# Sparse expert stage of an attention and mixture-of-experts layer: a rolled loop over resident weights against written-out tiles with weights brought per tile

## The chip, the cores and the metric

One core of one Trainium2 chip runs the whole program in one launch. The metric is device time in microseconds (us), the median of three runs.

## The reference

Input x is 2 x 1024 tokens of 128 channels, float32. The first half of the layer is causal attention with 16 heads and a layer norm around it. The second half, where the change lies, sends each token to 2 of 7 experts and to one shared expert:

```python
x_flat = layernorm(x).reshape(-1, 128)                    # 2048 tokens
logits = x_flat @ router_w.T                              # 7 experts
top_vals, top_idx = top_k(logits, 2);  top_w = softmax(top_vals)
swiglu(x, wg, wu, wd) = (silu(x @ wg) * (x @ wu)) @ wd    # 128 -> 512 -> 128, per expert
mixed = sum over the token's 2 experts of top_w * swiglu(x, expert) + swiglu(x, shared)
x = x + layernorm(mixed)
```

## The kernel before

The first block (lines up to 835) does the attention, the layer norms and the first half of the routing; both kernels do it alike. It ends near 378 us in the profile. The second block holds the rest of the layer:

- **Shared expert and routing.** The shared expert runs over 4 chunks of 512 tokens (`shared_up`, `shared_take`, `shared_down`, `shared_result`). Beside it VectorE (DVE) ranks the 4096 (token, expert) pairs by expert and writes two tables: `source` (which token stands in row p of tile k) and `target` (where its result goes), each 128 x 38. There are 38 tiles of 128 rows, each wholly of one expert. Which expert a tile belongs to is packed in `words`, one number for six tiles, three bits each. `places_ready` says that the tables are there, `words_ready` that the words are.
- **Weights.** At the start of the block SyncE (SP) issues 24 DMAs of 256 KB: gate, up and down weights of the shared expert and of all seven others, into `w_g`, `w_u`, `w_d`, where they stay.
- **Expert tiles.** For tile k: GpSimd (POOL) gathers 128 token rows from `tokens` in HBM by an indirect DMA (`gather`). TensorE (PE) transposes them (`turn`, L1164), ScalarE (ACT) copies the result to `rows_t`. PE multiplies them by gate and up weights (`up`, L1182, L1185): `rows_t` stands in the array and 512 weight columns move, so `hidden` comes out with tokens on partitions. ACT takes the silu, DVE the product (`hidden`, L1537). PE transposes `hidden` in four pieces (`turn_hidden`, L1173), ACT copies it (L1300), and PE multiplies it by the down weights (`project`, L1195). DVE copies the 128 x 128 result (L1545), and POOL scatters it to `results` in HBM (`scatter`).
- **Loops.** Each engine has a rolled loop (`Fori`). PE turns through six tiles at a time, reads a word into a register and takes the weights at a register's offset. The order on PE for tile k is turn(k+2), turn_hidden(k), up(k+1), project(k). Rows, hidden and results have two buffers each.
- **POOL's loop.** An indirect DMA takes its 128 row numbers from a column of SBUF. Since the column's place depends on the loop, POOL first copies it to `source_now` or `target_now` (L1018, L1030), waits for its own copy on `copied`, and then issues the DMA (L1021, L1033). Its order is gather(k+4), scatter(k).
- **End.** When all results are stored, SP brings them back in eight DMAs, they are weighted and added, and the last layer norm and the residual follow.

Of the kernel before, what the change touches and what calls it, by code (L numbers as in the profile page):

```python
# [25 lines left out]
P = 128  # L26
# [25 lines left out]
TAIL = 2  # L52
assert (TILES - TAIL) % PACK == 0 and PACK % 2 == 0
# [65 lines left out]
def program(nc, x, wqkv, wq_t, dirs, scales, w_out, router_t, w_gate, w_up, w_down, out):  # L119
    ctx = ExitStack()  # L120
    with ctx:
# [715 lines left out]
        w_g = sb("w_g", [C, NE, HID])  # L837
        w_u = sb("w_u", [C, NE, HID])
        w_d = sb("w_d", [P, NE, HT, C])
# [45 lines left out]
        source_now = [sb(f"source_now{i}", [P, 1], U32) for i in range(2)]  # L885
        target_now = [sb(f"target_now{i}", [P, 1], U32) for i in range(2)]
        rows = [sb(f"rows{i}", [P, C]) for i in range(2)]
        rows_t = [sb(f"rows_t{i}", [C, P]) for i in range(2)]
        gate = [sb(f"gate{i}", [P, HID]) for i in range(2)]
        hidden = [sb(f"hidden{i}", [P, HID]) for i in range(2)]  # L890
        hidden_t = [sb(f"hidden_t{i}", [P, HT, P]) for i in range(2)]
        result = [sb(f"result{i}", [P, C]) for i in range(2)]
# [5 lines left out]
        experts_loaded = sem("experts_loaded")  # L898
# [23 lines left out]
        rows_loaded = [sem(f"rows_loaded{i}") for i in range(2)]  # L922
        copied = sem("copied")
        offsets_in_place = sem("offsets_in_place")
# [6 lines left out]
        hidden_turned = sem("hidden_turned")  # L931
        hidden_t_ready = sem("hidden_t_ready")
        down_done = sem("down_done")
        result_ready = sem("result_ready")
        result_stored = [sem(f"result_stored{i}") for i in range(2)]
# [11 lines left out]
        PAIRS = (TILES - TAIL) // 2  # L947
        LAST = TILES - TAIL

        with nc.Block() as block:  # L950
            at_bank, pr_bank = [bank(0), bank(1)], [bank(2), bank(3)]
            g_bank, u_bank = [bank(0), bank(1)], [bank(2), bank(3)]
            xt_bank = turn_bank = [bank(4), bank(5)]
            d_bank, t_bank = bank(6), bank(7)
            cut = NT * 8
# [3 lines left out]

            @block.sync  # L960
            def _(sp):

                for e in [E] + list(range(E)):
                    loaded = shared_loaded if e == E else experts_loaded
                    sp.dma_start(w_g[:, e, :], w_gate[e]).then_inc(loaded, 16)
                    sp.dma_start(w_u[:, e, :], w_up[e]).then_inc(loaded, 16)
                    sp.dma_start(w_d[:, e, :, :], w_down[e].rearrange("(t p) c -> p t c", p=P)
                                 ).then_inc(loaded, 16)
# [4 lines left out]
                for i in range(2):  # L973
                    sp.wait_ge(result_stored[i], 16 * (TILES // 2))
# [16 lines left out]
            def _(pool):  # L991
# [22 lines left out]
                def gather(pair, u, count):  # L1014

                    k, i = pair * 2 + u, u % 2
                    pool.wait_ge(rows_turned, k + 1)
                    nc.gpsimd.tensor_copy(source_now[i][:, :], source[:, bass.ds(k, 1)]).then_inc(copied, 1)  # L1018
                    pool.wait_ge(copied, count)
                    pool.sem_inc(offsets_in_place, 1)  # L1020
# [5 lines left out]
                def scatter(pair, u, count):  # L1026

                    k, i = pair * 2 + u, u % 2
                    pool.wait_ge(result_ready, k + 1 + 1)
                    nc.gpsimd.tensor_copy(target_now[i][:, :], target[:, bass.ds(k, 1)]).then_inc(copied, 1)  # L1030
                    pool.wait_ge(copied, count)
                    pool.sem_inc(offsets_in_place, 1)
                    nc.gpsimd.indirect_dma_start(  # L1033
                        results, bass.IndirectOffsetOnAxis(ap=target_now[i][:, 0:1], axis=0),
                        result[i][:, :], None).then_inc(result_stored[i], 16)
# [3 lines left out]
                AHEAD = 4  # L1039
                for u in range(AHEAD):  # L1040
                    gather(0, u, u + 1)
                with pool.Fori(0, PAIRS - 1) as pair:
                    for u in range(2):
                        gather(pair, u + AHEAD, pair * 4 + (AHEAD + 2 * u + 1))
                        scatter(pair, u, pair * 4 + (AHEAD + 2 * u + 2))
                for u in range(AHEAD):
                    scatter(PAIRS - 1, u, (PAIRS - 1) * 4 + AHEAD + u + 1)

# [13 lines left out]
            def _(pe):  # L1062
                pe.sem_inc(rows_turned, CREDIT)

# [29 lines left out]
                def shared_up(q, ts):  # L1094
                    x_at = x2_t[:, q * CH:(q + 1) * CH, :].rearrange("c t p -> c (t p)")
                    for t in ts:
                        if q == CHUNKS - 1 and t >= 2:
                            pe.wait_ge(s_last_ready, t - 1)
                        elif q * HT + t >= 2:
                            pe.wait_ge(s_up_ready, q * HT + t - 1)  # L1100
                        nc.tensor.matmul(g_bank[t % 2], w_g[:, E, t * P:(t + 1) * P], x_at,
                                         start=True, stop=True).then_inc(s_gate_done, 1)
                        nc.tensor.matmul(u_bank[t % 2], w_u[:, E, t * P:(t + 1) * P], x_at,
                                         start=True, stop=True).then_inc(s_up_done, 1)

                def shared_down(q):
# [6 lines left out]
                    for j in range(CH):  # L1113
                        for t in range(HT):
                            last = nc.tensor.matmul(  # L1115
                                d_bank[:, j * P:(j + 1) * P],
                                s_hidden[q % 2][:, t, j * P:(j + 1) * P], w_d[:, E, t, :],
# [35 lines left out]
                def word(turn):  # L1153
                    return pe.value_load(words[0:1, bass.ds(turn, 1)], min_val=0, max_val=8 ** (PACK + 1) - 1)

                def digit(w, u):
                    return (w >> (3 * u)) & 7

                def turn(k, u):

                    i = u % 2
                    pe.wait_ge(rows_loaded[i], k * 8 + (u // 2 + 1) * 16)
                    pe.wait_ge(rows_t_ready, k + (u + 1))
                    nc.tensor.transpose(t_bank[:, i * P:(i + 1) * P], rows[i][:, :], ident[:, :]  # L1164
                                        ).then_inc(rows_turned, 1)

                def turn_hidden(k, u):

                    i = u % 2
                    pe.wait_ge(hidden_ready, k + (u + 1 + CREDIT))  # L1170
                    pe.wait_ge(hidden_t_ready, k + (u + 1))
                    for t in range(HT):
                        last = nc.tensor.transpose(turn_bank[i][:, t * P:(t + 1) * P],  # L1173
                                                   hidden[i][:, t * P:(t + 1) * P], ident[:, :])
                    last.then_inc(hidden_turned, 1)

                def up(k, u, e):

                    i = u % 2
                    pe.wait_ge(rows_t_ready, k + (u + 1 + 1))  # L1180
                    pe.wait_ge(hidden_ready, k + (u + 1))
                    nc.tensor.matmul(g_bank[i], rows_t[i][:, :],  # L1182
                                     w_g[:, bass.ds(e, 1), :].rearrange("c e h -> c (e h)"),
                                     start=True, stop=True).then_inc(gate_done, 1)
                    nc.tensor.matmul(u_bank[i], rows_t[i][:, :],  # L1185
                                     w_u[:, bass.ds(e, 1), :].rearrange("c e h -> c (e h)"),
                                     start=True, stop=True).then_inc(up_done, 1)

                def project(k, u, e):

                    i = u % 2
                    pe.wait_ge(hidden_t_ready, k + (u + 1 + CREDIT))
                    pe.wait_ge(result_ready, k + (u + 1))
                    for t in range(HT):
                        last = nc.tensor.matmul(d_bank[:, 0:P], hidden_t[i][:, t, :],  # L1195
                                                w_d[:, bass.ds(e, 1), t, :].rearrange("p e c -> p (e c)"),
# [4 lines left out]
                turn(0, 0)  # L1201
                turn(0, 1)
                shared_down(CHUNKS - 1)
                pe.wait_ge(words_ready, 1)
                pe.wait_ge(experts_loaded, 16 * 3 * E)
                first_expert = digit(word(0), 0)
                up(0, 0, first_expert)
                pe.wait_ge(s_down_taken, CHUNKS)
                with pe.Fori(0, (TILES - TAIL) // PACK) as n:
                    w, k = word(n), n * PACK  # L1210
                    for u in range(PACK):
                        turn(k, u + 2)
                        turn_hidden(k, u)
                        up(k, u + 1, digit(w, u + 1))
                        project(k, u, digit(w, u))
                w = word(WORDS - 1)
                turn_hidden(LAST, 0)
                up(LAST, 1, digit(w, 1))
                project(LAST, 0, digit(w, 0))
                turn_hidden(LAST, 1)  # L1220
                project(LAST, 1, digit(w, 1))

# [390 lines left out]
```

## Time and profile before

| | |
|---|---|
| device time, median of 3 runs (lowest to highest) | 625.59 us (623.78 to 627.57) |
| profiled execution, first to last instruction | 621.6 us |
| mean granted TensorE clock, share of full speed | 0.950 |
| busy over the span: PE, DVE, ACT, POOL | 490.9, 356.5, 287.1, 141.3 us |
| DMA over the span | 27.38 MB, mean 44 GB/s |
| first gather issued; first matmul of tile 0 | 432.82 us; 441.40 us |
| last result of tile 37 copied; result DMAs read back from | 591.67 us; 595.34 us |

The times of the profile are from one profiled execution, in us from its first instruction. Its span is 4.0 us under the median of the runs, which also hold what lies around the first and last instruction. "PE" is TensorE's matmul track, "PEld" its weight loads. A float32 matmul shows as two PE instructions.

### The profile page before, as it was taken

To read this page: it belongs to the slowest core of one execution; us is meant where nothing else is said; L and a number is where in the kernel's file an instruction comes from. 1 tells how busy PE (TensorE), PEld (TensorE's weight loads), DVE (VectorE), ACT (ScalarE), POOL (GpSimd) and SP (SyncE) were. 2 spreads that over 40 slices of the span, in tenths; PEclk is the share of its full clock that TensorE was granted. 3 is DMA by queue.
4 is the path that set the end of the run, shared out by engine and by line. 5 is a ranking of instruction groups with operands and counts; after the bars stand their busy time and mean duration, and the time that the engine had idled before them with its cause. 6 is when DMAs were issued, how large, how long until landed. Compare 5 with 4: busy or idle time off the path is not lost. (4 is left out here: it accounts for less than half of the span.)

```text
span 621.6 us, 12143 instructions
## 1 busy us (share of the span) xinstructions
PE 490.9 (79%) x3660; PEld 261.3 (42%) x3661; DVE 356.5 (57%) x936; ACT 287.1 (46%) x639; POOL 141.3 (23%) x214
## 2 busy tenths in 40 slices
PE   1636789898994999989898987888888889888800
PEld 0421234443442434444443445555555556555500
DVE  4966988686873767868673662688222212222247
ACT  0330045665753657565575765752333333333321
POOL 9310000000000000000000001424365556655424
PEclk9987889999998999999999997999999999999965
DMA  3066030210303003030000005900011111111152
GB/s 89 4 152 152 1 55 3 39 18 7 50 4 57 2 3 55 3 53 4 3 1 3 2 1 181 294 1 4 21 33 34 34 33 30 34 34 34 25 143 67
DMA packets 31930, 27.38 MB, mean 44 GB/s; under 512 B 7723, under 2 KB 25516, under 8 KB 31852
## 3 DMA queue, kind: packets, MB, share of 16 engines
q1 hardware_dynamic: 29444, 21.71, 15.2%
q0 software_dynamic: 2432, 4.99, 3.0%
q8 instruction: 29, 0.48, 0.3%
q14 instruction: 25, 0.20, 0.1%
HBM read 18.55 MB, written 7.73 MB: 42 GB/s over the span
## 5 line engine op out<-in xcount | busy, mean ns | idle before, releaser
L703 DVE TENSOR_REDUCE mx_part<-banks 128x1 f32<-128x512 f32 (+3 forms) x384 | 194.9, 552 | 79.0 <-PE banks L426 38.9
L608 ACT ACTIVATE probs<-banks 128x512 f32<-128x512 f32 (+3 forms) x384 | 164.6, 496 | 134.9 <-PE banks L445 134.2
L426 PE MATMUL banks<-k_st,q_st 128*128 128x512 bf16 (+3 forms) x384 | 126.8, 341 | 24.7 <-DMA k_st<-k_parts 13.7
L441 PE MATMUL banks<-q_st,k_st 128*128 128x512 bf16 (+3 forms) x384 | 117.2, 332 | 9.4 <-ACT probs L608 4.5
L463 PE MATMUL banks<-probs,v_pad 128*32 128x256 f32 (+1 forms) x1280 | 95.4, 370 | 13.0 <-ACT probs L608 13.0
L1537 DVE TENSOR_TENSOR hidden<-banks,gate 128x512 f32<-128x512 f32 x38 | 26.3, 691 | 108.9 <-PE banks L1185 108.9
L426 PEld LDWEIGHTS banks<-k_st,q_st 128*128 128x128 bf16 x384 | 37.4, 98 | 82.8 <-DVE mx_part L703 43.7
L441 PEld LDWEIGHTS banks<-q_st,k_st 128*128 128x128 bf16 x384 | 36.9, 97 | 68.5 <-ACT probs L608 46.3
L359 POOL COPY v_pad<-v_all 128x256 f32 (+1 forms) x8 | 3.7, 479 | 246.4 <-PE banks L463 229.7
L429 PE MATMUL banks<-mask_qk,ident_b 128*128 128x128 bf16 x256 | 56.2, 224 | 0.0
L445 PE MATMUL banks<-mask_kq,ident_b 128*128 128x128 bf16 x256 | 52.8, 220 | 0.0
L1195 PEld LDWEIGHTS banks<-w_d,hidden_t 128*128 128x128 f32 x304 | 39.8, 191 | 18.7 <-issue 18.7
L463 PEld LDWEIGHTS banks<-probs,v_pad 128*32 128x32 f32 x1280 | 25.3, 107 | 49.3 <-ACT probs L608 24.4
L1033 POOL DMA_INDIRECT results<-result,target_now x38 | 37.7, 993 | 31.0 <-POOL target_now L1030 31.0
L1021 POOL DMA_INDIRECT rows<-tokens,source_now x38 | 38.0, 999 | 30.0 <-POOL source_now L1018 26.0
L1288 ACT ACTIVATE rows_t<-banks 128x128 f32<-128x128 f32 x38 | 10.5, 278 | 72.2 <-PE banks L1164 72.2
L1195 PE MATMUL banks<-w_d,hidden_t 128*128 x304 | 40.1, 275 | 0.8 <-ACT hidden_t L1300 0.8
L1182 PE MATMUL banks<-w_g,rows_t 128*128 x76 | 40.6, 616 | 0.0
L1185 PE MATMUL banks<-w_u,rows_t 128*128 x76 | 38.8, 592 | 0.0
L1164 PE MATMUL banks<-ident,rows 128*128 128x128 f32 x38 | 12.0, 315 | 21.4 <-DMA rows<-tokens,source_now 21.3
L1295 ACT ACTIVATE gate<-banks 128x512 f32<-128x512 f32 x38 | 22.7, 597 | 11.7 <-PE banks L1182 11.7
L1300 ACT ACTIVATE hidden_t<-banks 128x512 f32<-128x512 f32 x38 | 22.7, 597 | 10.7 <-PE banks L1173 10.7
(202 smaller groups left out, 550.3 us busy)
## 6 DMA issues: line engine op xcount, KB each, us to landing
q_st<-q_parts SPq DMA_DIRECT2D x48, 64.0 KB
w_g<-in_w_gate SPq DMA_DIRECT2D x8, 256.0 KB, 5.4
w_u<-in_w_up SPq DMA_DIRECT2D x8, 256.0 KB, 5.6
w_d<-in_w_down SPq DMA_DIRECT2D x8, 256.0 KB, 5.9
back<-results SPq DMA_DIRECT2D x8, 256.0 KB, 5.0
q_parts<-probs SPq DMA_DIRECT2D x12, 128.0 KB, 3.3
k_parts<-probs SPq DMA_DIRECT2D x12, 128.0 KB, 3.3
k_st<-k_parts SPq DMA_DIRECT2D x8, 192.0 KB
```

What stands on the lines that cost most here:

```text
L426: last = nc.tensor.matmul(dst[:, 0:z - a], q_st[r][:, h, i * P:(i + 1) * P], k_st[r][:, h, a:z], start=True, stop=(z < width))
L429: last = nc.tensor.matmul(dst[:, z - a - P:z - a], ident_b[:, :], mask_qk[:, :], start=False, stop=True)
L441: last = nc.tensor.matmul(dst[:, 0:z - a], k_st[r][:, h, j * P:(j + 1) * P], q_st[r][:, h, j * P + a:j * P + z], start=True, stop=(a > 0))
L445: last = nc.tensor.matmul(dst[:, 0:P], ident_b[:, :], mask_kq[:, :], start=False, stop=True)
L463: last = nc.tensor.matmul(o_bank[c][h * HQ:(h + 1) * HQ, a - c * BANK:z - c * BANK], v_pad[r][:, j, h, :], probs[j % 2][:, h, a - j * P:z ...
L608: nc.scalar.activation(probs[j % 2][:, h, a:z], score_bank[k % RING][:, 0:z - a], ACT.Exp).then_inc(slot_taken, 1)
L703: nc.vector.tensor_reduce(mx_part[r][:, h * KT + i, s:s + 1], max_bank[k % RING][:, 0:z - a], AX.X, ALU.max).then_inc(max_taken, 1)
L1021: nc.gpsimd.indirect_dma_start(rows[i][:, :], None, tokens, bass.IndirectOffsetOnAxis(ap=source_now[i][:, 0:1], axis=0)).then_inc(rows_loa ...
L1033: nc.gpsimd.indirect_dma_start(results, bass.IndirectOffsetOnAxis(ap=target_now[i][:, 0:1], axis=0), result[i][:, :], None).then_inc(resul ...
L1182: nc.tensor.matmul(g_bank[i], rows_t[i][:, :], w_g[:, bass.ds(e, 1), :].rearrange("c e h -> c (e h)"), start=True, stop=True).then_inc(gat ...
L1185: nc.tensor.matmul(u_bank[i], rows_t[i][:, :], w_u[:, bass.ds(e, 1), :].rearrange("c e h -> c (e h)"), start=True, stop=True).then_inc(up_ ...
L1195: last = nc.tensor.matmul(d_bank[:, 0:P], hidden_t[i][:, t, :], w_d[:, bass.ds(e, 1), t, :].rearrange("p e c -> p (e c)"), start=(t == 0), ...
```

## The change

The 38 tiles are written out on every engine instead of looped. What each part does:

- SP loads only the shared expert's weights at the start of the block (`s_w_g`, `s_w_u`, `s_w_d`). After `words_ready` it reads each tile's expert number into a register and issues three DMAs of 256 KB per tile into one of three sets of fixed buffers. The set of tile k is written again once project(k-3) is done (`down_done`). Before up(k), PE waits for all three of the tile.
- The offsets of gathers and scatters are read in place from `source` and `target`; the copies and their waits are gone. Rows and results have four buffers. POOL's order is gather(k+3), scatter(k), after the first four gathers.
- In `up` the weights stand and the rows move: four 128 x 128 matmuls for gate, four for up. `hidden` comes out with hidden units on partitions, so `turn_hidden` and ACT's copy are gone.
- The order on PE for tile k is turn(k+2), up(k+1), project(k). The turned rows and the results have two banks each.

```diff
+        w_d = [sb(f"w_d{i}", [P, HT, C]) for i in range(WEIGHTS)]      # WEIGHTS = 3, ROWS = 4
...
             def _(sp):
-                for e in [E] + list(range(E)):
-                    loaded = shared_loaded if e == E else experts_loaded
-                    sp.dma_start(w_g[:, e, :], w_gate[e]).then_inc(loaded, 16)
...
+                sp.wait_ge(words_ready, 1)
+                for k, e in enumerate(digits(sp)):
+                    i = k % WEIGHTS
+                    if k >= WEIGHTS:
+                        sp.wait_ge(down_done, k - WEIGHTS + 1)
+                    sp.dma_start(w_g[i][:, :], w_gate[bass.ds(e, 1), :, :].rearrange("e c h -> c (e h)")
+                                 ).then_inc(weights_in[i], 16)
+                    sp.dma_start(w_u[i][:, :], w_up[bass.ds(e, 1), :, :].rearrange("e c h -> c (e h)")
+                                 ).then_inc(weights_in[i], 16)
+                    sp.dma_start(w_d[i][:, :, :], w_down[bass.ds(e, 1), :, :].rearrange(
+                        "e (t p) c -> p (e t) c", p=P)).then_inc(weights_in[i], 16)
...
-                def gather(pair, u, count):
-                    k, i = pair * 2 + u, u % 2
-                    pool.wait_ge(rows_turned, k + 1)
-                    nc.gpsimd.tensor_copy(source_now[i][:, :], source[:, bass.ds(k, 1)]).then_inc(copied, 1)
-                    pool.wait_ge(copied, count)
+                def gather(k):
+                    i = k % ROWS
+                    if k >= ROWS:
+                        pool.wait_ge(rows_turned, k - ROWS + 1)
                     nc.gpsimd.indirect_dma_start(
                         rows[i][:, :], None, tokens,
-                        bass.IndirectOffsetOnAxis(ap=source_now[i][:, 0:1], axis=0)
+                        bass.IndirectOffsetOnAxis(ap=source[:, k:k + 1], axis=0)
                     ).then_inc(rows_loaded[i], 16)
+                def scatter(k):
+                    i = k % ROWS
+                    pool.wait_ge(result_ready, k + 1)
                     nc.gpsimd.indirect_dma_start(
+                        results, bass.IndirectOffsetOnAxis(ap=target[:, k:k + 1], axis=0),
                         result[i][:, :], None).then_inc(result_stored[i], 16)
...
+                for k in range(ROWS):
+                    gather(k)
+                for k in range(TILES):
+                    if ROWS <= k + ROWS - 1 < TILES and k > 0:
+                        gather(k + ROWS - 1)
+                    scatter(k)
...
+                def up(k):
+                    i = k % WEIGHTS
+                    pe.wait_ge(weights_in[i], 48 * (k // WEIGHTS + 1))
+                    pe.wait_ge(rows_t_ready, k + 1)
+                    if k >= 2:
+                        pe.wait_ge(hidden_ready, k - 1)
+                    for w, dst, sem_done in ((w_g, g_bank, gate_done), (w_u, u_bank, up_done)):
+                        for t in range(HT):
+                            last = nc.tensor.matmul(dst[k % 2][:, t * P:(t + 1) * P], w[i][:, t * P:(t + 1) * P],
+                                                    rows_t[k % 2][:, :], start=True, stop=True)
+                        last.then_inc(sem_done, 1)
...
+                turn(0)
                 shared_down(CHUNKS - 1)
+                turn(1)
                 pe.wait_ge(words_ready, 1)
+                up(0)
                 pe.wait_ge(s_down_taken, CHUNKS)
+                for k in range(TILES):
+                    if k + 2 < TILES:
+                        turn(k + 2)
+                    if k + 1 < TILES:
+                        up(k + 1)
+                    project(k)
```

## Rows read from the trace of the kernel before

**Rows 1.** Windows: PE, PEld, DVE, ACT, POOL busy us (instructions), clock, DMA share, GB/s.
```profile
459.00:579.00 120.00, 102.75 (x515) 68.20 (x515) 29.50 (x60) 44.33 (x91) 71.96 (x121) 1.00 0.12 33
```

**Rows 2.** Chain that ended last, around 514 us: start, duration, what.
```profile
513.94 0.21 POOL source_now L1018
...
514.19 0.52 issue
...
514.93 2.52 DMA rows<-tokens,source_now
...
517.57 0.34 PE banks L1164
```

**Rows 3.** Timeline from 447 us, one tile on PE: start, duration, idle before.
```profile
447.33 0.27 PE L1164 MATMUL banks<-ident,rows 128*128 128x128 f32 x1
...
447.45 0.66 PE L1173 MATMUL banks<-ident,hidden 128*128 128x128 f32 x4
...
447.95 1.04 PE L1182 MATMUL banks<-w_g,rows_t 128*128 x2
...
449.68 1.05 PE L1195 MATMUL banks<-w_d,hidden_t 128*128 x8
...
450.57 0.27 PE L1164 MATMUL banks<-ident,rows 128*128 128x128 f32 x1
...
450.77 0.29 DVE L1545 COPY result<-banks 128x128 f32<-128x128 f32 x1
```

**Rows 4.** SP's own issues in time: weights at 378 us, register-addressed attention loads, results back.
```profile
378.44 0.37 SPq L965 DMA_DIRECT2D w_g<-in_w_gate  x1
...
379.33 0.43 SPq L967 DMA_DIRECT2D w_d<-in_w_down  x1
...
117.96 2.37 SPq L278 DMA_DIRECT2D q_st<-q_parts  x6
...
595.34 0.36 SPq L978 DMA_DIRECT2D back<-results  x1
...
596.29 0.51 SPq L978 DMA_DIRECT2D back<-results  x1
```

**Rows 5.** DMA view, single issues: the first w_g, the first w_d, the third back.
```profile
w_g<-in_w_gate SPq DMA_DIRECT2D x1, 256.0 KB, 2.9
...
w_d<-in_w_down SPq DMA_DIRECT2D x1, 256.0 KB, 5.0
...
back<-results SPq DMA_DIRECT2D x1, 256.0 KB, 4.2
```

**Rows 6.** DMA view, 378 to 386 us (instruction queue) and 380 to 402 us.
```profile
q8 instruction: 1, 0.02, 0.7%
...
DMA packets 8550, 7.30 MB, mean 332 GB/s; under 512 B 413, under 2 KB 6530, under 8 KB 8546
```

**Rows 7.** Tile view of rows: issue of a gather to its landing.
```profile
DMA to landing us min/median/max: 2.5/2.6/3.5
```

**Rows 8.** Timeline, 431 to 438 us: tables ready, first copy, words, last shared chunk.
```profile
431.72 0.19 POOL L1018 COPY source_now<-source 128x1 uint32<-128x1 uint32 x1 [6.97 <-issue]
...
432.85 0.17 DVE L1521 CAST words<-words_f 1x7 uint32<-1x7 f32 x1
...
435.91 0.69 DVE L1476 TENSOR_TENSOR s_hidden<-banks,s_gate 128x512 f32<-128x512 f32 x1 [1.38 <-ACT s_gate L1253]
...
437.81 3.75 PE L1115 MATMUL banks<-w_d,s_hidden 128*128 128x128 f32 x32
```

**Rows 9.** Timeline, end of the tiles: the last result, and POOL behind it.
```profile
591.67 0.29 DVE L1545 COPY result<-banks 128x128 f32<-128x128 f32 x1 [2.23 <-PE banks L1195]
592.03 0.18 POOL L1030 COPY target_now<-target 128x1 uint32<-128x1 uint32 x1 [0.56 <-DVE result L1545]
```

**Rows 10.** Windows of 4 us: where the granted clock fell, and a stalled tile.
```profile
374.00:378.00 4.00, 1.79 (x8) 1.39 (x8) 0.62 (x2) 1.84 (x5) 0.00 (x0) 0.68 0.00 0
...
458.00:462.00 4.00, 2.98 (x15) 2.00 (x16) 0.34 (x1) 1.47 (x3) 2.40 (x5) 1.00 0.12 33
```

More of the change, by code:

```diff
@@ L51 @@
 PADDED = (WORDS + 1) * PACK
-TAIL = 2
-assert (TILES - TAIL) % PACK == 0 and PACK % 2 == 0
+WEIGHTS = 3
+ROWS = 4
 CH = BANK // P
@@ L832, in program @@
         front.close()
-        w_g = sb("w_g", [C, NE, HID])
-        w_u = sb("w_u", [C, NE, HID])
-        w_d = sb("w_d", [P, NE, HT, C])
+        s_w_g = sb("s_w_g", [C, HID])
+        s_w_u = sb("s_w_u", [C, HID])
+        s_w_d = sb("s_w_d", [P, HT, C])
+        w_d = [sb(f"w_d{i}", [P, HT, C]) for i in range(WEIGHTS)]
+        w_g = [sb(f"w_g{i}", [C, HID]) for i in range(WEIGHTS)]
+        w_u = [sb(f"w_u{i}", [C, HID]) for i in range(WEIGHTS)]
         proj = sb("proj", [P, KT, C])
@@ L884, in program @@
         s_hidden = [sb(f"s_hidden{i}", [P, HT, BANK]) for i in range(2)]
-        source_now = [sb(f"source_now{i}", [P, 1], U32) for i in range(2)]
-        target_now = [sb(f"target_now{i}", [P, 1], U32) for i in range(2)]
-        rows = [sb(f"rows{i}", [P, C]) for i in range(2)]
+        rows = [sb(f"rows{i}", [P, C]) for i in range(ROWS)]
         rows_t = [sb(f"rows_t{i}", [C, P]) for i in range(2)]
         gate = [sb(f"gate{i}", [P, HID]) for i in range(2)]
-        hidden = [sb(f"hidden{i}", [P, HID]) for i in range(2)]
-        hidden_t = [sb(f"hidden_t{i}", [P, HT, P]) for i in range(2)]
-        result = [sb(f"result{i}", [P, C]) for i in range(2)]
+        hidden = [sb(f"hidden{i}", [P, HT, P]) for i in range(2)]
+        result = [sb(f"result{i}", [P, C]) for i in range(ROWS)]
         root_table = sb("root_table", [P, 1])
@@ L921, in program @@
         s_down_taken = sem("s_down_taken")
-        rows_loaded = [sem(f"rows_loaded{i}") for i in range(2)]
-        copied = sem("copied")
-        offsets_in_place = sem("offsets_in_place")
+        weights_in = [sem(f"weights_in{i}") for i in range(WEIGHTS)]
+        rows_loaded = [sem(f"rows_loaded{i}") for i in range(ROWS)]
         rows_turned = sem("rows_turned")
@@ L958, in program, with digits @@
             rank_bank = t_bank[:, 2 * P + 3 * TILES:2 * P + 3 * TILES + E * NT]
+            def digits(engine):
+                for n in range(WORDS):
+                    word = engine.value_load(words[0:1, n:n + 1], min_val=0, max_val=8 ** (PACK + 1) - 1)
+                    for u in range(min(PACK, TILES - n * PACK)):
+                        yield (word >> (3 * u)) & 7
             @block.sync
             def _(sp):
-                for e in [E] + list(range(E)):
-                    loaded = shared_loaded if e == E else experts_loaded
-                    sp.dma_start(w_g[:, e, :], w_gate[e]).then_inc(loaded, 16)
-                    sp.dma_start(w_u[:, e, :], w_up[e]).then_inc(loaded, 16)
-                    sp.dma_start(w_d[:, e, :, :], w_down[e].rearrange("(t p) c -> p t c", p=P)
-                                 ).then_inc(loaded, 16)
+                sp.dma_start(s_w_g[:, :], w_gate[E]).then_inc(shared_loaded, 16)
+                sp.dma_start(s_w_u[:, :], w_up[E]).then_inc(shared_loaded, 16)
+                sp.dma_start(s_w_d[:, :, :], w_down[E].rearrange("(t p) c -> p t c", p=P)
+                             ).then_inc(shared_loaded, 16)
                 for b in range(B):
@@ L1038, in _ @@
                 pool.wait_ge(places_ready, 2)
[L1039 to L1047, printed above, removed]
+                for k in range(ROWS):
[4 more added lines that the diff above has]
+                    scatter(k)
                 for q in range(QC, CHUNKS):
@@ L1116, in shared_down @@
                                 d_bank[:, j * P:(j + 1) * P],
[L1117 removed]
+                                s_hidden[q % 2][:, t, j * P:(j + 1) * P], s_w_d[:, t, :],
                                 start=(t == 0), stop=(t == HT - 1))
@@ L1151, in _ @@
                 shared_up(3, [1, 2, 3])
[L1153 to L1164, printed above, removed]
-                                        ).then_inc(rows_turned, 1)
@@ L1167, in turn_hidden @@
[L1167 to L1171, printed above, removed]
-                    for t in range(HT):
[L1173 to L1196, printed above, removed]
+                def turn(k):
+                    i = k % ROWS
+                    pe.wait_ge(rows_loaded[i], 16 * (k // ROWS + 1))
+                    if k >= 2:
+                        pe.wait_ge(rows_t_ready, k - 1)
+                    nc.tensor.transpose(turn_bank[k % 2][:, 0:P], rows[i][:, :], ident[:, :]
+                                        ).then_inc(rows_turned, 1)
@@ L1197, in project @@
+                def project(k):
+                    pe.wait_ge(hidden_ready, k + 1)
+                    if k >= 2:
+                        pe.wait_ge(result_ready, k - 1)
+                    for t in range(HT):
+                        last = nc.tensor.matmul(down_bank[k % 2][:, 0:P], hidden[k % 2][:, t, :],
+                                                w_d[k % WEIGHTS][:, t, :],
                                                 start=(t == 0), stop=(t == HT - 1))
@@ L1200, in _ @@
                 pe.wait_ge(places_ready, 2)
-                turn(0, 0)
-                turn(0, 1)
+                pe.wait_ge(x2_t_ready, CHUNKS)
+                turn(0)
                 shared_down(CHUNKS - 1)
+                turn(1)
                 pe.wait_ge(words_ready, 1)
-                pe.wait_ge(experts_loaded, 16 * 3 * E)
-                first_expert = digit(word(0), 0)
-                up(0, 0, first_expert)
+                up(0)
                 pe.wait_ge(s_down_taken, CHUNKS)
[L1209 to L1221, printed above, removed]
+                for k in range(TILES):
[4 more added lines that the diff above has]
+                    project(k)
             @block.scalar
             def _(act):
-                act.sem_inc(rows_t_ready, 1)
-                act.sem_inc(hidden_t_ready, CREDIT)
                 for half in range(2):
@@ L1531, in _, with multiply, take_result @@
                                         ).then_inc(weight_ready, 1)
-                def multiply(pair, u):
-                    k, i = pair * 2 + u, u % 2
+                def multiply(k):
                     dve.wait_ge(gate_ready, k + 1)
                     dve.wait_ge(up_done, k + 1)
-                    nc.vector.tensor_tensor(hidden[i][:, :], u_bank[i], gate[i][:, :], ALU.mult
-                                            ).then_inc(hidden_ready, 1)
-                def take_result(pair, u, first=False):
-                    k, i = pair * 2 + u, u % 2
-                    dve.wait_ge(down_done, k + 1)
-                    if not first:
-                        dve.wait_ge(result_stored[i], pair * 16)
-                    nc.vector.tensor_copy(result[i][:, :], d_bank[:, 0:P]).then_inc(result_ready, 1)
-                multiply(0, 0)
-                for u in range(2):
-                    multiply(0, u + 1)
-                    take_result(0, u, first=True)
-                with dve.Fori(1, PAIRS) as pair:
-                    for u in range(2):
-                        multiply(pair, u + 1)
-                        take_result(pair, u)
-                multiply(PAIRS, 1)
-                for u in range(2):
-                    take_result(PAIRS, u)
+                    if k >= 2:
+                        dve.wait_ge(down_done, k - 1)
+                    nc.vector.tensor_tensor(hidden[k % 2][:, :, :].rearrange("p t n -> p (t n)"), u_bank[k % 2],
+                                            gate[k % 2][:, :], ALU.mult).then_inc(hidden_ready, 1)
+                def take_result(k):
+                    i = k % ROWS
+                    dve.wait_ge(down_done, k + 1)
+                    if k >= ROWS:
+                        dve.wait_ge(result_stored[i], 16 * (k // ROWS))
+                    nc.vector.tensor_copy(result[i][:, :], down_bank[k % 2][:, 0:P]).then_inc(result_ready, 1)
+                multiply(0)
+                for k in range(TILES):
+                    if k + 1 < TILES:
+                        multiply(k + 1)
+                    take_result(k)
                 dve.wait_ge(s_down_taken, CHUNKS)
```

71 lines of the change are left out of this document (25 added, 46 removed).

## The prediction

> **What bounds the kernel now.** I read the windows first. In the steady part of the tiles no engine looks full: PE is busy 103 of 120 us, POOL 72, DMA 12% [rows 1]. Busy share alone would name PE. The chain that ended last says otherwise: it runs through POOL's copy, an "issue" stretch and the indirect DMA, over and over, and PE appears only for a transpose released by a landed gather [rows 2]. The reader should see a latency loop inside POOL: copy starts 513.94, indirect DMA starts 514.93, so 0.99 us pass before the DMA's own 1.00 us. Two such per tile (gather, scatter) make 3.98 us, and 120 us / 3.98 is 30 tiles, the count of POOL's 121 instructions over four. The stretch of 0.52 us is POOL's sequencer preparing the indirect DMA. It cannot run ahead now, because it waits for the copy.
>
> PE alone needs less. Where gathers were ahead, a tile took it 450.57 - 447.33 = 3.24 us [rows 3]: transpose of rows 0.12, of hidden 0.50, gate and up 1.73, down 0.89. So POOL costs 0.75 us a tile over PE, and that is all that freeing POOL alone could give: 28 us over 38 tiles.
>
> **The change, part by part.**
>
> POOL. Without copies the sequencer can prepare one indirect DMA while the other executes, so POOL's own floor is two executions, 2.0 us a tile. Preparation still counts where POOL was waiting: from the end of the copy to the start of the DMA, 514.93 - (513.94 + 0.21) = 0.78 us [rows 2].
>
> PE. `turn_hidden` goes: -0.50. `up` becomes 8 float32 matmuls of 128 columns. Such a matmul costs 0.89 / 4 = 0.22 us in `project` (449.68 to 450.57) [rows 3], so 8 cost 1.78 against 1.73. Per tile 0.12 + 1.78 + 0.89 = 2.79 us. ACT loses a copy off the path. Nothing moves to DVE.
>
> The gather's round trip. gather(k+4) is issued behind scatter(k), and turn(k+4) is PE's next instruction after project(k+1). Call P(k) the end of project(k). DVE starts its copy 1.09 us after project's start, so P + 0.20, and takes 0.29 [rows 3]. Then 592.03 - 591.96 = 0.07 for the semaphore [rows 9], 0.78 preparation, 1.00 for the scatter, then gather to the transpose 517.57 - 514.93 = 2.64 [rows 2]. Together 0.20 + 0.29 + 0.07 + 0.78 + 1.00 + 2.64 = 4.98. Then turn, up and project, 2.79. So P(k+2) is at least P(k) + 7.77: two tiles per round trip.
>
> The weights' round trip. This is new, and SP, which issued nothing here, now issues 114 DMAs. The three of tile k+3 start when P(k) is seen, and up(k+3) comes after P(k+1) and the turn. Behind that waiting PE instruction stand project(k+2), and behind it DVE's copy and POOL's scatter. The loop is 0.20 + 0.07, then L, the time from the first issue to the third landing, 0.13 to wake PE, up and project 2.67: 3.07 + L per two tiles. L is the disputed number. From the first weights: first issued 378.44 [rows 4], third issued 379.33 and landed 5.0 later [rows 5], L = 5.9. In that time a block of instructions passed through one of the 16 DMA engines and held it 0.7% x 16 x 8 us = 0.9 us [rows 6], so undisturbed it would have been about 5.0. From the results read back at the end: third issued 596.29, landed 4.2 later, from 595.34: L = 5.15 [rows 4, 5], in smaller pieces. From below: the first DMA lands 2.9 after issue [rows 5], and 256 KB at the sustained 332 GB/s is 0.79 us [rows 6], so 2.9 + 2 x 0.79 = 4.5. I take 4.9, nearest to the undisturbed load, and 0.1 for the scatter that shares the engines: 3.07 + 5.0 = 8.07, say 8.05 per two tiles, 4.03 a tile. Register-addressed issue adds nothing visible: six such took 2.37 us, 0.39 each, no more than the static ones [rows 4]. Bandwidth is no bound: 3 x 0.79 = 2.4 us of 4 and the row traffic at 12% of 4 us, 0.5.
>
> On L the Trainium skill speaks for the change. Its page "DMA: Bandwidth & Descriptors", section "Anatomy of one DMA", fits a DMA from GpSimd as about 2.0 us plus bytes at 436 GB/s. By it the three, issued within 0.9 us, would be down after some 3.8 us, and the weights would never set the pace. The first w_g took 2.9 where the rule gives 2.6; the third disagrees more.
>
> Start. words is ready at 433.02 [rows 8]; 9 DMAs go out, and the first set lands by about 433.1 + 4.9 = 438, hidden behind the last shared chunk. The first gather starts about 0.4 us sooner (no copy), and `shared_down` no longer waits for the second gather: it starts when DVE's last product is there, 435.91 + 0.69 = 436.6 instead of 437.81 [rows 8]. 32 instructions at 0.11 end at 440.2; then turn(1) and up(0) to 442.1; turn(2), up(1), project(0): P(0) = 442.1 + 2.79 = 444.95. P(1) is 2.8 later.
>
> Middle. P(36) = 444.95 + 18 x 8.05 = 589.85; the last project follows directly, 0.95 later: P(37) = 590.8. Before, DVE's last copy started at 591.67 [rows 9], so P(37) was 591.47: -0.7.
>
> End. One copy and its wait less before the last scatter, -0.2.
>
> Instruction blocks. Written-out code is fetched once through the same DMA engines. A block held one engine 0.9 us [rows 6]. I estimate up to 15 blocks; each can delay one set of weights, on one of two interleaved chains (odd and even tiles), and only if it falls in the 2.4 of 4 us when they move: between 0 and 7 us, I take +1.5.
>
> Everything else in the block is unchanged. The 21 resident loads that go from 380 to 402 us stood beside a chain on DVE that did not wait for them: 0.
>
> Sum: -0.7 - 0.2 + 1.5 = +0.6 on 621.6, 622.2; with the 4.0 us by which the median of the runs stands above the profiled span, 626.2. I say 626.5.
>
> **The rivals.**
>
> Faster: the loads come down in under 4.6 us, and the gathers' round trip of 7.77 paces the stage. P(37) = 444.95 + 18 x 7.77 + 0.95 = 585.8, so -5.7 - 0.2 on the median: 619.7. For it: the lower bound of 4.5, and bursts that no longer queue behind 20 others. Against it: both observed L are above 5. A leaner preparation of the indirect DMA (0.5 instead of 0.78) would give 5 us more.
>
> Slower, one mechanism: the three loads take 5.9 us as observed, because gathers, scatters and instruction blocks share their engines each time. 3.07 + 5.9 = 8.97; P(37) = 445.9 + 161.5 = 607.4, +15.9 - 0.2: 641.3. It decides from L = 5.2 (8.27 and the 1.5 give more than 3.1 us). Gathers have landed as late as 3.5 us against a median of 2.6 [rows 7], so single DMAs do vary by 1 us.
>
> Clock: PE would be busy 5.6 of 8 us, 70%, with gaps of over 2 us. The granted clock fell where PE was busy 1.79 of 4 us, and not where it was busy 2.98 of 4 around a 2 us gap [rows 10]. At half clock a tile costs PE 5.6 us, 36 x 5.6 = 201: some 57 us more, 684. Unlikely.
>
> PE-bound: both round trips hidden, 2.79 a tile: 36 x 2.79 = 100 instead of 145, 580. The gather rows exclude it nearly.
>
> Loops: the skill's page "Runtime: NRT & Kernel Launch", section "Instruction fetch mechanics", says that a taken branch can force a fetch and that writing out avoids it. Here the loops' turns cost nothing on the path, as POOL held its 3.98 us throughout.
>
> **How the numbers follow.** A difference of 0.5%, 3.1 us, is about what a measurement can tell from no change. My case (weights' round trip, 7.9 to 8.3 us per two tiles; 622 to 631 us) 0.47, of it 0.05 faster, 0.32 same, 0.10 slower. Gather-paced 0.22, slow loads 0.27, clock 0.03, PE-bound 0.01. Faster 0.28, same 0.32, slower 0.40. The range 617.5 to 641 takes in the leaner gather partly and L up to 5.9; the likeliest case alone is 622 to 631.
>
> **What would show it.** After: no L1018 or L1030 copies, indirect DMAs of one tile back to back on POOL, POOL busy near half; PE waits before the first `up` matmul released by a w_d landing, every second tile (waits before the transpose by rows would mean the gathers pace); windows in which DMA is 65 to 75% busy at about 225 GB/s; first to third landing 4.9 to 5.1; 8.05 us per two tiles. The prediction is wrong if the third load lands outside 4.6 to 5.2 us, if the two weight DMAs of neighbouring tiles queue on each other, or if the clock drops.

## The result and the profile after

The changed kernel takes 659.59 us (median of 4 runs, 659.41 to 665.79) against 625.06 of before, measured beside it: ratio 1.0571, 95% interval 1.0523 to 1.062. It is 5.7% slower, outside the stated range of 617.5 to 641. The profiled execution spans 657.6 us, 36.0 more than before and 35.4 more than the 622.2 of the prediction's sum.

Windows of 20 us of the changed kernel, columns as in [rows 1]:

```profile
480.00:500.00 20.00, 14.87 (x100) 14.49 (x100) 3.68 (x9) 3.50 (x8) 7.78 (x8) 0.83 0.59 178
500.00:520.00 20.00, 14.68 (x100) 14.49 (x100) 3.84 (x8) 3.50 (x8) 7.59 (x9) 0.83 0.58 177
```

A tile has 25 PE instructions (1 + 16 + 8), so 100 in 20 us are four tiles: 5.0 us a tile, against POOL's 3.98 of before. The granted clock is 0.83, where it was 1.00 [rows 1]. Neither PE, nor POOL, nor DMA (0.59) is full.

The chain that ended last, one turn of it:

```profile
487.12 0.30 DVE result L1509
487.42 0.27 issue
487.69 0.99 POOL results L1037
488.67 0.30 issue
488.98 3.50 DMA rows<-tokens,source
492.48 0.04 issue
492.52 0.33 PE banks L1157
492.85 3.19 PE banks L1169 x16
496.05 1.14 PE banks L1178 x8
497.18 0.02 issue
497.21 0.30 DVE result L1509
```

This is the gathers' round trip, link by link: result copied, scatter, gather, landing, turn, `up`, `project`. It takes 497.21 - 487.12 = 10.09 us and moves two tiles. The weights do not appear in it. The timeline of the same stretch:

```profile
486.92 0.27 PE L1157 MATMUL banks<-ident,rows 128*128 128x128 f32 x1
487.02 1.06 PE L1169 MATMUL banks<-rows_t,w_g 128*128 128x128 f32 x8
...
492.52 0.33 PE L1157 MATMUL banks<-ident,rows 128*128 128x128 f32 x1 [2.66 <-DMA rows<-tokens,source]
...
492.69 1.65 PE L1169 MATMUL banks<-rows_t,w_g 128*128 128x128 f32 x8
...
494.13 1.91 PE L1169 MATMUL banks<-rows_t,w_u 128*128 128x128 f32 x8
```

The reader should see two things. PE idles 2.66 us in front of every second transpose, released by landed rows. And the eight instructions that took 1.06 us in the first tile take 1.65 to 1.91 in the tile after the gap. Windows of a few us show why:

```profile
489.00:492.50 3.50, 0.87 (x8) 0.68 (x7) 0.98 (x2) 0.00 (x0) 2.66 (x3) 1.00 1.02 325
492.50:496.00 3.50, 3.48 (x18) 3.48 (x19) 0.00 (x0) 0.88 (x2) 0.24 (x1) 0.57 0.55 174
496.00:499.00 3.00, 3.00 (x27) 3.00 (x26) 0.98 (x2) 0.87 (x2) 0.99 (x1) 0.93 0.09 16
```

In the first, PE is idle and the DMA engines are completely busy (1.02): the weights of a tile are moving while the rows wait for their turn. In the second, PE works at a granted clock of 0.57, that is, mostly at 1.2 GHz. In the third it is back near 2.4 GHz and the DMA engines are nearly idle (0.09). So the mean DMA share of 0.59 hides bursts at 100%, and the gather is issued into the burst.

The landing times, from the tile views of rows, w_g and w_d (issue to landing; [rows 5, 7] for before):

```profile
DMA to landing us min/median/max: 2.7/3.6/5.7
...
DMA to landing us min/median/max: 2.5/2.9/4.0
...
DMA to landing us min/median/max: 3.4/3.9/5.8
```

Rows land 1.0 us later than before (2.6). The third weight DMA is issued 0.9 us behind the first (490.11 and 491.01 in the timeline), so first issue to third landing is 4.8 us.

### The profile page after: what moved, and what is told of

Same layout as the page of the kernel before. It is cut to its first block and busy times, and to the rows that moved or that the text cites. A ratio compares the mean times of both kernels' runs of the same rounds, so it can differ in the third digit from the quotient of the medians.

```text
span 657.6 us, 12058 instructions
## 1 busy us (share of the span) xinstructions
PE 500.3 (76%) x3964; PEld 310.3 (47%) x3964; DVE 354.8 (54%) x936; ACT 264.3 (40%) x601; POOL 125.1 (19%) x138
## 5 line engine op out<-in xcount | busy, mean ns | idle before, releaser
L1037 POOL DMA_INDIRECT results<-result,target x38 | 37.5, 986 | 111.6 <-DVE result L1509 111.3
L1262 ACT ACTIVATE rows_t<-banks 128x128 f32<-128x128 f32 x38 | 10.5, 278 | 117.4 <-PE banks L1157 117.4
L1169 PE MATMUL banks<-rows_t,w_u 128*128 128x128 f32 x304 | 52.0, 329 | 0.0
L1169 PE MATMUL banks<-rows_t,w_g 128*128 128x128 f32 x304 | 47.9, 309 | 2.3 <-DMA w_d<-in_w_down 2.3
L1157 PE MATMUL banks<-ident,rows 128*128 128x128 f32 x38 | 12.5, 328 | 48.3 <-DMA rows<-tokens,source 48.3
L1169 PEld LDWEIGHTS banks<-rows_t,w_u 128*128 128x128 f32 x304 | 48.5, 243 | 0.0
L1178 PE MATMUL banks<-w_d,hidden 128*128 128x128 f32 x304 | 47.2, 307 | 0.0
L1169 PEld LDWEIGHTS banks<-rows_t,w_g 128*128 128x128 f32 x304 | 43.9, 222 | 2.9 <-DMA w_d<-in_w_down 2.7
L1178 PEld LDWEIGHTS banks<-w_d,hidden 128*128 128x128 f32 x304 | 44.7, 226 | 0.1
L1029 POOL DMA_INDIRECT rows<-tokens,source x38 | 36.9, 972 | 20.6 <-issue 11.3
```

What stands on the lines that cost most here:

```text
L1029: nc.gpsimd.indirect_dma_start(rows[i][:, :], None, tokens, bass.IndirectOffsetOnAxis(ap=source[:, k:k + 1], axis=0)).then_inc(rows_loaded ...
L1037: nc.gpsimd.indirect_dma_start(results, bass.IndirectOffsetOnAxis(ap=target[:, k:k + 1], axis=0), result[i][:, :], None).then_inc(result_s ...
L1169: last = nc.tensor.matmul(dst[k % 2][:, t * P:(t + 1) * P], w[i][:, t * P:(t + 1) * P], rows_t[k % 2][:, :], start=True, stop=True)
L1178: last = nc.tensor.matmul(down_bank[k % 2][:, 0:P], hidden[k % 2][:, t, :], w_d[k % WEIGHTS][:, t, :], start=(t == 0), stop=(t == HT - 1))
```

## The experiments

A is the theory that the weight traffic delays the gathers, B that the granted clock makes up the loss, C that the weights' round trip paces. E1 to E4 ran on one chip, E5, E6, E9 and E10 on one, E11 and E12 on one. E1, E2, E3, E5, E6 and E12 have one time each; their spans are compared with the 657.6 of the changed kernel. How far single runs scatter is seen from the kernel before, whose 21 runs beside the experiments took 619.96 to 629.16 us, with medians of 623.66, 624.78 and 624.42 on the three chips; a few us of one run are no finding by themselves. The time of the tiles alone, at the end of this section, scatters less.

**E1: no weight DMAs after tile 2.**

```diff
                     if k >= WEIGHTS:
-                        sp.wait_ge(down_done, k - WEIGHTS + 1)
+                        break
...
-                    pe.wait_ge(weights_in[i], 48 * (k // WEIGHTS + 1))
+                    pe.wait_ge(weights_in[i], 48)
```

> Left out: the weight DMAs of tiles 3 to 37 (the buffers keep the weights of tiles 0 to 2, so the results are of the wrong expert). Two tiles now take 10.1 us, 5.65 from the end of a project to the transpose of the rows four tiles on, and 4.45 for transpose, up and project. Theory A (the gathers share the DMA engines with the weights): landing falls from 3.6 to 2.6 us, the wait to 4.65; two tiles take 9.1 if the clock still falls each time, 7.5 if it no longer does: 640 or 611 us of span. Theory B (only the clock): landing stays 3.6, no gain unless the clock stays up. Theory C (the weights' own round trip paces): the wait on the weights goes, about the same gain as A, but the landing of the rows stays 3.6.

Measured: 627.61 us, span 625.6, 32.0 less. The rows' median landing is 2.7 us. Its chain:

```profile
503.44 0.30 DVE result L1509
503.75 0.27 issue
504.01 0.98 POOL results L1037
505.00 0.30 issue
505.30 2.53 DMA rows<-tokens,source
507.84 0.04 issue
507.88 0.33 PE banks L1157
508.21 1.79 PE banks L1169 x16
510.00 0.91 PE banks L1178 x8
510.91 0.02 issue
510.93 0.30 DVE result L1509
```

The same links take 510.93 - 503.44 = 7.49 us. Landing fell from 3.50 to 2.53, and `up` from 3.19 to 1.79: with the shorter gaps the clock mostly stays up (0.96 from 470 to 590 us). A holds and C falls, for the path still runs through the rows. The gain lies between the two cases that A gave, as some turns still lose the clock: behind its four gaps of 2.01 to 2.37 us the next tile took PE 4.23 to 4.48 us, behind those of up to 1.77 us about 3.0.

**E2: filler matmuls in PE's gap.**

```diff
                 for k in range(TILES):
+                    if 0 < k < TILES - 2:
+                        for _ in range(5):
+                            nc.tensor.matmul(turn_bank[k % 2][:, 2 * P:3 * P], ident[:, :], x2_t[:, 0, :],
+                                             start=True, stop=True)
                     if k + 2 < TILES:
                         turn(k + 2)
```

> Added: five float32 matmuls of 128 columns (1.1 us at full clock) in front of each rows transpose, into an unused part of a bank. They fit in the gap of 2.7 us that PE has in every second tile, and add nothing to what the path needs: 2 x (2.79 + 1.1) = 7.8 is under the present 10.1. Theory B (the granted clock halves because PE stands idle, and that costs 1.7 us per two tiles): clock 1.00 through the stage, two tiles take 5.65 + 2.79 = 8.45, span 657.6 - 18 x 1.65 = 628. Theory A alone (the clock does not matter): no gain, or 1.1 us lost per tile where PE was not waiting.

Measured: 638.87 us, span 637.1, 20.5 less with more work. The window from 470 to 590 us:

```profile
470.00:590.00 120.00, 108.54 (x939) 105.44 (x939) 26.55 (x54) 23.63 (x54) 51.50 (x53) 1.00 0.66 205
```

The clock is 1.00. B holds in kind, but the gain is 1.1 us per two tiles and not 1.65: the rows' landings in its chain from 490 to 515 us are 3.24, 4.67, 3.40 and 4.60 us (mean 4.0), against 3.62, 4.57, 3.17, 3.58, 3.50 and 3.93 (mean 3.7) in the changed kernel's chain from 447 to 500 us. More is moved in the same time (205 GB/s against 181 in the same window of the changed kernel); that this is what lengthens the landings is argued, no run shows it alone.

**E5: both.** No weight DMAs after tile 2, and the filler.

> Left out: the weight DMAs of tiles 3 to 37 (results of the wrong expert); added: the filler matmuls. Both costs named by A and B are then gone: rows land in 2.6 us and the clock is full. The gathers' round trip is 0.2 + 0.3 + 0.27 + 1.0 + 0.3 + 2.6 + 2.8 = 7.5 us per two tiles, PE with filler 7.8: span 616 to 620. If a third cost is at work, it stays at 625 or more.

Measured: 618.75 us, span 617.0, as expected. PE with its filler now sets the pace: from one transpose of rows to the next are 3.91 us in most turns, and PE waits for rows only five times. So the two costs together are worth at least 657.6 - 617.0 = 40.6 us. They are not additive (32.0 + 20.5 = 52.5), because the clock falls on account of the gap that the late rows make. No third cost is needed to explain this time; one hidden under PE's 3.91 us would not show.

**E3: eight row and result buffers.**

```diff
-ROWS = 4
+ROWS = 8
```

> Eight row and result buffers in place of four, so a gather is issued seven tiles ahead. Theory A+B (the round trip scatter to gather to transpose paces): PE no longer waits for rows; what is left is the weights' round trip, 3.07 + 4.8 = 7.9 us per two tiles at full clock, 9.5 with the clock falling: 618 to 646. Theory C (weights pace now): no change, 658.

Measured: 646.38 us, span 643.6, 14.0 less. The waits from 460 to 540 us (who waits <- for whom: us in all, times, the longest in us):

```profile
PE banks L1169 <- DMA w_d<-in_w_down: 20.7, 10, 3.3
```

PE no longer waits for rows; it waits for the third weight DMA. The path that I had forecast is real, but lies just behind the one that paced. The chain also holds one piece of 7.72 us from 436.26 for which no releaser is named, in front of the first `up`; E4 has more of that kind.

**E6: the gather in front of the scatter.** Four buffers as in the changed kernel.

```diff
-                    if ROWS <= k + ROWS - 1 < TILES and k > 0:
-                        gather(k + ROWS - 1)
+                    if k + ROWS < TILES:
+                        gather(k + ROWS)
                     scatter(k)
```

> One line of POOL's order changed: the gather of tile k+4 is issued before the scatter of tile k, not behind it. Buffers stay four and three. If the gather is late only because it stands behind a scatter that waits for the result, PE no longer waits for rows and the kernel falls to the pace of the weights' round trip, as with eight buffers: span 640 to 646. If four buffers are too few in themselves, it stays near 658.

Measured: 650.02 us, span 647.7, 9.9 less, near the expected 640 to 646 but not in it. From 490 to 530 us its chain holds landings of w_d and none of rows, and from 440 to 632 us PE waits 41.9 us for w_d and never for rows (48.3 us in the changed kernel). So the gathers came late for the scatter that they stood behind, which itself waited for a result.

**E12: eight buffers and the filler.**

> Eight row buffers and the filler matmuls: the gathers are off the path and the clock is held, so the weights' round trip of the prediction stands alone. By it, 3.07 us plus the first-to-third landing (4.8 in the changed kernel, 5.2 with eight buffers): 7.9 to 8.3 us per two tiles, span 622 to 629. If the round trip is longer than its parts, or PE waits elsewhere, it stays near 643.

Measured: 636.46 us, span 634.7, missed by 6 us. The clock is 1.00, and PE waits only for w_d, now as the chain shows:

```profile
482.69 0.02 issue
...
483.90 4.78 DMA w_d<-in_w_down
488.68 0.04 issue
488.72 2.05 PE banks L1169 x16
490.77 0.91 PE banks L1178 x8
```

This turn is 491.68 - 482.69 = 8.99 us: 483.00 to 488.68 for the three DMAs (5.7 where the medians give 5.0), and 2.05 + 0.91 for PE after a wait where I had 1.78 + 0.89. In the mean a turn takes 8.7 us (17 turns in 148.16 us). The weights' round trip was undersized too: this turn was set by loads that came later than the median; the latest w_d landed 5.8 us after its issue, the median one 4.1.

**E9: POOL's part alone in the kernel before.** Weights resident, all other loops kept. The gather and the loop are shown; the scatter is changed in the same way.

```diff
-                    nc.gpsimd.tensor_copy(source_now[i][:, :], source[:, bass.ds(k, 1)]).then_inc(copied, 1)
-                    pool.wait_ge(copied, count)
-                    pool.sem_inc(offsets_in_place, 1)
                     nc.gpsimd.indirect_dma_start(
                         rows[i][:, :], None, tokens,
-                        bass.IndirectOffsetOnAxis(ap=source_now[i][:, 0:1], axis=0)
+                        bass.IndirectOffsetOnAxis(ap=source[:, k:k + 1], axis=0)
...
-                with pool.Fori(0, PAIRS - 1) as pair:
...
+                for k in range(TILES - AHEAD):
+                    gather(k + AHEAD)
+                    scatter(k)
```

> The kernel before, with POOL's gathers and scatters alone written out and their offsets read in place; every other engine keeps its loop, the weights stay resident. PE's own 3.24 us a tile should pace in place of POOL's 3.99: (3.99 - 3.24) x 31 = 23 us off, span about 599, time about 602. If POOL were not what paced the kernel before, no change.

Measured: 599.02 us, ratio 0.9588 (0.9548 to 0.9629), span 597.0. The forecast of the kernel before as bound by POOL's copies was right, and the path is now PE alone:

```profile
506.71 0.11 PE banks L1157
506.82 0.52 PE banks L1166 x4
507.33 0.87 PE banks L1175 x2
508.20 0.86 PE banks L1178 x2
509.06 0.89 PE banks L1188 x8
509.95 0.11 PE banks L1157
```

509.95 - 506.71 = 3.24 us a tile, as [rows 3] gave it.

**E4: eight row and result buffers, six weight sets.**

> Eight row and result buffers and six weight sets. No round trip is left. Either PE at full clock paces, 2.79 us a tile, or the DMA engines, 2.4 + 0.5 = 2.9 a tile: P(37) near 551, span about 582 to 586, time about 588, faster than both kernels. If instead the DMA queue cannot keep several sets in flight under the row traffic (theory D: bandwidth and contention pace), 3.3 us a tile or more: 600 or above.

Measured: 598.46 us, ratio 0.9604 (0.9546 to 0.9663), span 593.5: faster than both kernels, but 10.5 us over the 588 expected. The DMA share is 0.88 to 1.06 in the windows from 440 to 540 us, and the chain has five pieces like this one, 24 us in all:

```profile
435.82 7.71 another core or an unknown queue
...
495.55 4.21 another core or an unknown queue
```

In four of the five ScalarE, and in the one at 479.75 (3.90 us) VectorE, waits for nothing that the profile can name; no other core runs. I suspected blocks of instructions, which come through the same DMA engines. The view of the DMA queues does not bear this out: it has a packet of the instruction queue in the first of the five stretches and none in the other four. The cause stays open.

**E10: down weights resident.** In `project` they are the moving operand and can be addressed by a register. Six sets of gate and up weights, the gather first, four row buffers.

```diff
+                for e in range(E):
+                    sp.dma_start(w_d[:, e, :, :], w_down[e].rearrange("(t p) c -> p t c", p=P)
+                                 ).then_inc(downs_loaded, 16)
...
-                        sp.wait_ge(down_done, k - WEIGHTS + 1)
+                        sp.wait_ge(up_done, k - WEIGHTS + 1)
...
-                                                w_d[k % WEIGHTS][:, t, :],
+                                                w_d[:, bass.ds(e, 1), t, :].rearrange("p e c -> p (e c)"),
```

> The changed kernel with the down weights resident (they are the moving operand, so a register can address them), six sets of gate and up weights, and the gather before the scatter. Per tile 0.5 MB instead of 0.8: 1.6 + 0.5 = 2.1 us of the DMA engines against 2.8 of PE. PE should pace: P(37) near 547, span about 577, time about 581. Theory D (with the DMA engines full, engines wait for their own instruction blocks, as ACT did for 4.2 us with six full sets): the stalls should go with the load on the DMA engines; if they stay, span about 593 as there.

Measured: 599.57 us, ratio 0.9582 (0.9525 to 0.9638); the 581 was missed by 18.6 us. The profiled run spans 599.9. Its chain again has rows landing in it, 3.0 to 5.2 us after issue. I had forgotten the four buffers: gather(k+4) still follows scatter(k-1). Two stalls without a named releaser are left in the chain, 2.06 and 1.34 us, where E4 had five of 3.9 to 7.7; the DMA share is 0.61 to 0.64 from 460 to 540 us.

**E11: E10 with eight buffers.**

> As e10 (down weights resident, six sets of gate and up, gather first), with eight row and result buffers. e10 missed its 577 because with four buffers and 2.8 us a tile a gather still has only two tiles, 5.6 us, from the scatter in front of it to its transpose, and rows took 3.5 to 5 us to land. With eight that wait goes; if nothing else is at work, PE paces: span 577 to 582. If the stalls without a named releaser (ACT and DVE, up to 4 us each) remain, 585 to 592.

Measured: 578.16 us, ratio 0.9268 (0.9221 to 0.9315), span 576.5, the fastest of all. The window from 480 to 540 us:

```profile
480.00:540.00 60.00, 60.00 (x540) 60.00 (x539) 21.24 (x43) 18.83 (x43) 37.54 (x39) 1.00 0.72 210
```

PE is never idle; from one transpose of rows to the next are 2.79 us, as forecast. The rows still land after 4.3 us (median), which costs nothing with this lead: the gather issued at 469.58 is that of tile 17, whose transpose starts at 484.25, 14.7 us later.

**The tiles alone.** A span also holds what lies in front of the tiles, and that varied by some 5 us between these single profiles. The timelines give the stretch from the start of the transpose of tile 3's rows to that of tile 37's, 17 turns:

| run | from | length | less than the changed kernel |
|---|---|---|---|
| changed kernel | 445.84 | 173.22 | |
| E1, no weight DMAs | 450.15 | 139.02 | 34.2 |
| E2, filler | 447.09 | 152.73 | 20.5 |
| E5, both | 445.66 | 135.89 | 37.3 |
| E3, eight buffers | 449.17 | 155.84 | 17.4 |
| E6, gather first | 450.28 | 158.78 | 14.4 |
| E12, eight buffers and filler | 449.21 | 148.16 | 25.1 |
| E11 | 445.20 | 94.83 | 78.4 |

The order of the runs is the same as by span. E1, E3, E6 and E12 gained 2 to 5 us more in the tiles than their spans tell, because their tiles began 3.3 to 4.4 us later; E6's small miss is no larger than that.

## Why the prediction was wrong

**POOL before, 3.98 us a tile:** right. E9 took it away and got PE's 3.24.

**PE's 2.79 us a tile:** right at full clock; E11 runs at it.

**The start:** P(0) was forecast for 444.95 and came at 445.84. Of these 0.9 us, 0.4 had gone before turn(2), which began at 442.47 and not 442.1, and 0.5 went to the wait for the weights of tile 1, which landed at 443.02. **The end:** from the last result copy to the end 29.4 us, 0.5 less than before; forecast 0.2.

**The gathers' round trip, the step that failed.** I had 7.77 us per two tiles, less than the 8.05 of the weights' round trip, and so let the weights pace. It measured 10.09 and paced itself, with the sign that I had named for that case: PE waits before the transpose for rows. Term by term, from the chain above:

| term | predicted | measured |
|---|---|---|
| project's end to result copied | 0.49 | 0.32 |
| preparation and semaphore before the scatter | 0.85 | 0.27 |
| scatter | 1.00 | 0.99 |
| between scatter and gather | 0 | 0.30 |
| gather's start to landing | 2.52 | 3.50 |
| waking PE, and the transpose | 0.24 | 0.37 |
| `up` and `project` | 2.67 | 4.33 |
| sum | 7.77 | 10.08 |

On POOL the terms erred both ways: the preparation costs 0.27 without the copy, not 0.78 after it, but 0.30 stands between two indirect DMAs. Two terms make the loss. The landing: I charged the weights' traffic to the loads (0.1 for the scatter) and never to the gather, whose landing I took from a kernel with DMA at 12%. And PE's part: +1.66, nearly all the clock. Over 18 turns this is 18 x (10.06 - 8.05) = 36.2 us, with 10.06 the mean from P(0) = 445.84 to P(36) = 626.85. With 0.9 for the start, 0.15 for the last project, -0.3 for the end and -1.5 for the instruction blocks that did not show, it gives the miss of 35.4 within 0.1 us.

The Trainium skill, page "DMA: Bandwidth & Descriptors", section "Issuing engines are not separate DMA queues", says that DMAs of SP and GpSimd interleave on the same 16 engines. The traces agree with it: the same gather lands after 3.6 us beside the weight traffic, 2.6 before, and 2.7 in E1 without it.

**The weights' round trip, 8.05.** L = 4.9 was right at the median (4.8), the pacing was not: in the changed kernel this loop is not on the path, and in E12, where it paces, a turn takes 8.7 us in the mean, since late loads and PE's start after a wait lengthen it. The Trainium skill, page "DMA: Bandwidth & Descriptors", section "Anatomy of one DMA", fits a DMA issued by GpSimd as 2.0 us plus bytes at 436 GB/s; an estimate from it is 3.8 us for L. The trace, at 4.8 for loads issued by SP, does not agree.

**The clock, given a chance of 0.03.** I reasoned from a busy share of 70% and from one stall that had done no harm [rows 10]; I called it 2 us there, it was 1.81, shorter than every gap of the changed kernel's turns. In the changed kernel PE stood idle 2.3 to 4.4 us in front of every second transpose, and behind 16 of these 17 gaps the next tile took it 4.2 to 5.2 us instead of 2.8. The clock did not halve for everything, as my rival had it, but only for one tile in two: 1.66 us of the turn above; taking it away in E2 gave back 1.1. The rival that I had priced was the wrong shape: the loss feeds on the gap that another wait makes.

**The rivals.** "The gathers' round trip paces" (0.22) named the path that paced, but at the price of 7.77, and so forecast a gain (619.7). "Loads take 5.9" came nearest in sum (641.3) for a wrong reason. **Instruction blocks, +1.5:** the view of the DMA queues has 7 such packets from 440 to 628 us where I had up to 15 blocks, and nothing on the path shows them.

## What to carry to other kernels

Price a loop of waits with the traffic that the change itself adds: a small DMA's latency read from a quiet kernel did not hold here beside bursts at 100% (3.6 us against 2.6), even though the mean DMA share was 0.6. When a round trip leaves PE a gap of 2 to 3 us in each turn, as here, count the matmuls behind the gap at the lower clock. And give transfers whose addresses are known a place in front of those that wait for results, with enough buffers; here that, with six sets of gate and up weights and the down weights resident, turned +5.7% into -7.3%.

## What the runs showed of the hardware

- An indirect DMA whose offsets need no copy started 0.27 us after its wait ended, or 0.30 us after the end of the one before it.
In E1 it fell behind the four gaps of 2.0 to 2.4 us and not behind those of up to 1.8. With the filler in the gaps (E2) it stayed at 2.4 GHz from 470 to 590 us.
- With the DMA engines 88 to 106% busy, ScalarE stalled up to 7.7 us and VectorE 3.9 us with no releaser that the profile names (E4). With 54 to 93% (E11) no such stall is on the path. The cause is open.
